# Cross-attention values with the transposed probabilities as weights, in a one-core transformer block

## The chip, the cores and the metric

One Trainium2 chip, one of its cores. The metric is the device time of one execution in microseconds (us). Engines are named as the profile names them: PE is TensorE's products, PEld its weight loads, DVE is VectorE, ACT ScalarE, POOL GpSimd, and SP the engine that issues the DMAs.

## The reference, cut to what matters

A block on x of (8, 256, 1024), float32: grouped-query self-attention with sign weights, cross-attention to a context of (8, 256, 1024), and a low-rank gated feed-forward part, each behind a layernorm and added to x. The part that matters here:

```python
C_q, C_kv = Q @ Wq_d, K @ Wkv_d                       # 1024 -> 128, 1024 -> 64
CqWqk = (C_q @ W_qk).reshape(b, n, 16, 64)
scores = einsum('bnhl,bkl->bhnk', CqWqk, C_kv) / 8
attn = softmax(scores, axis=-1)                       # 256 keys a sequence
V_up = (C_kv @ Wv_u).reshape(b, nkv, 16, 64)
out = einsum('bhnk,bkhd->bnhd', attn, V_up)           # added to x
```

## The kernel before

Three phases follow one another: self-attention, cross-attention, feed-forward. One list, `ORDER`, is written out by hand (`self_order`, `cross_order`, `ffn_order`), and every engine's program goes through it and emits its own instructions of each step, with semaphore waits ahead of them. So the place of a step in `ORDER` is its place in the queue of each engine that takes part in it, SP's and POOL's among them; an engine does nothing out of that order.

**Cross-attention** goes over four groups g of 512 tokens (two sequences b), and in each over eight units j, U = 8g + j: two heads (r = 0, 1) of 64 columns by two sequences, four "heads" n = 4U to 4U + 3 in the code's count, written k0 to k3 here. Steps of a group ahead of the heads: `lowq`, `xq` (queries of a unit), `lowkv`, `vup` (values). Then `attention_order` (L62) writes the heads. In the step of head n it puts, in this order:

- `score` of head n + 3: PE (L819), four products into one of three score banks; DVE takes the maximum (L1298).
- `flip` n: PE transposes the probabilities, four blocks of 128x128 (L831).
- `exp` n + 1: ACT (L1032), with the row sums. `evac` n: copy of the transposed probabilities to SBUF, `probT`, on ACT for odd n (L1041), on DVE for even n (L1306).
- what is left of the side pieces of the step before (`rest`), and the first part of this step's own. Side pieces of a unit: at k0 and k3 a `turn` (PE, L696) of the next group's tiles, whose `split` (high half by ACT L991, low half by DVE L1199, out of the same bank) comes one step later, at k1 and k0; at k0 the layernorm statistics of a tile (DVE L1187 to L1193, POOL L1473, L1475); at k1, for j up to 5, `xq` of unit j + 2 (PE L885), whose `xq_out` comes at k2: ACT L1063, DVE L1357, and four DMAs of SP into `xq_stack` (L1636), on which `score` of that unit's first head waits, at k1 of the next unit; at k3 the load of a tile. The last group has no turns and splits.
- the finish of the unit before (`finish`, L93): at k1 `xcopy`: ACT copies the bank `attn` (values, heads and columns on partitions, tokens along the free axis) to `xattnT` (L1078). At k2 `xfin`: PE turns it into one of two `proj` banks (four transposes, L904); then `xfin_out`: DVE multiplies by the reciprocal sums into `tmp` (L1382), POOL adds that to `x_group` (L1514), SP stores it (L1642) and reloads the slice of the unit before that for the next group (L1646).
- after odd heads, that is at k2 and at the next k0, `values` for b = 0 and b = 1 (L834 to L849).

`values` has the value columns as weights (128 keys x 64) and the transposed probabilities moving (256 queries). Its products for r = 0 and r = 1 go to the halves of the array's columns:

```python
t = pe.matmul(attn[r * XD:(r + 1) * XD, b * SEQ:(b + 1) * SEQ],
              xv[:, b * QT + kt, (2 * j + r) * XD:(2 * j + r + 1) * XD],   # weights
              probT[n % 6][:, kt * SEQ:(kt + 1) * SEQ], ..., tile_position=(0, r * XD))
```

The first `values` of a unit waits until `xcopy` of the unit before has read `attn` (`xcopied`). What a group's last unit leaves to finish (`late`) stands behind the next group's `lowq`, or at the end of the phase, which waits for the last stores. The `proj` banks are handed out in the order of `ORDER` (`bank_uses`) to all steps of the table `BANKED`, `turn`, `xq` and `xfin` among them. A float32 product is recorded as two pieces, each with its weight load; a transpose or a product of the type float32r as one. Line 707, which the prediction refers to, makes a float32 product with 128x128 weights of ones and 128 moving columns.

Of the kernel before, what the change touches and what calls it, by code (L numbers as in the profile page):

```python
# [5 lines left out]
F32 = mybir.dt.float32  # L6
# [55 lines left out]
def attention_order(first, heads, side, lead):  # L62
# [8 lines left out]
    for n in range(heads + 1):  # L71
        if n + AHEAD < heads:
            order.append(("score", first + n + AHEAD))
        if n < heads:
            order.append(("flip", first + n))
            if n + 1 < heads:
                order.append(("exp", first + n + 1))
            order.append(("evac", first + n))
        order += rest
        rest = []  # L80
        for piece in side.get(n, []):
            order.append(piece[0])
            rest += piece[1:]
        if finish:
            order += finish.pop(0)
        if n >= 1:
            m = n - 1
            if m % 2 == 1:
                order.append(("values", (first + m) // 2))
            if m % XUH == XUH - 1:  # L90
                unit = (first + m) // XUH
                order.append(("xend", unit))
                finish += [[("xcopy", unit)], [("xfin", unit), ("xfin_out", unit)]]  # L93
# [193 lines left out]
def ffn_order():  # L287
# [54 lines left out]
    for i in range(2 * TILES):  # L342
# [9 lines left out]
          "lowkv": "lowkv_out", "xq": "xq_out", "vup": "vup_out", "xfin": "xfin_out", "b1": "b1_out",  # L352
# [79 lines left out]
def build_program(nc, x, ctx_in, wq, qs, wk, ks, wv, vs, wo, os_, wq_d, w_qk, wkv_d, wv_u,  # L432
# [3 lines left out]
    def sb(name, shape, dt, where=ctx):  # L436
        return where.enter_context(nc.sbuf_tensor(name, shape, dt))

    def semaphore(name):
# [53 lines left out]
            for i, ph in enumerate("yc")}  # L493
# [10 lines left out]
    OTs = [sb(f"xattnT{i}", [P, GT], F32, mem) for i in range(2)]  # L504
# [34 lines left out]
             "xv_dve xv_act xrecip xcopied xnormed xadded "  # L539
# [21 lines left out]
    def copied_out(kind, *at):  # L561
# [25 lines left out]
        if kind == "xfin_out":  # L587
            return sem["xnormed"], at[0] + 1
# [76 lines left out]
    def tensor_program(e):  # L665
        pe = e.eng
        for kind, *at in ORDER:
# [166 lines left out]
            elif kind == "values":  # L834
# [5 lines left out]
                if b == 0 and U:  # L840
                    e.wait_ge(sem["xcopied"], U)
                for kt in range(QT):
                    for r in range(2):
                        n = 2 * s + r
                        e.wait_ge(evacuated[n % 2], n // 2 + 1)
                        t = pe.matmul(attn[r * XD:(r + 1) * XD, b * SEQ:(b + 1) * SEQ],  # L846
                                      xv[:, b * QT + kt, (2 * j + r) * XD:(2 * j + r + 1) * XD],
                                      probT[n % 6][:, kt * SEQ:(kt + 1) * SEQ], start=kt == 0, stop=kt == QT - 1,
                                      tile_position=(0, r * XD))  # L849
# [37 lines left out]
            elif kind == "vup":  # L887
# [9 lines left out]
                t.then_inc(full, 1)  # L897
            elif kind == "xfin":
                U = at[0]
                J, full, use = bank_of("xfin_out", U)  # L900
                e.wait_ge(sem["xcopied"], U + 1)
                bank_free(e, "xfin_out", U)
                for a in range(TILES):
                    t = pe.transpose(J[:, a * P:(a + 1) * P], OTs[U % 2][:, a * P:(a + 1) * P], ident[:, :])  # L904
# [60 lines left out]
    def scalar_program(e):  # L965
        act = e.eng
        for kind, *at in ORDER:
# [104 lines left out]
            elif kind == "xcopy":  # L1072
                U = at[0]
                e.wait_ge(sem["valued"], (U + 1) * GB)
                if U > 1:
                    _, full, use = bank_of("xfin_out", U - 2)
                    e.wait_ge(full, use + 1)
                act.activation(OTs[U % 2][:, :], attn[:, :], ACT.Copy).then_inc(sem["xcopied"], 1)  # L1078
# [72 lines left out]
    def vector_program(e):  # L1151
        dve = e.eng
        for kind, *at in ORDER:
# [220 lines left out]
            elif kind == "xfin_out":  # L1374
                U = at[0]
                J, full, use = bank_of("xfin_out", U)
                heads4 = lambda a: a.rearrange("p (a r d) -> p a r d", a=TILES, r=2)
                e.wait_ge(full, use + 1)
                e.wait_ge(sem["xrecip"], U + 1)
                if U > 1:  # L1380
                    e.wait_ge(sem["xadded"], U - 1)
                t = dve.tensor_tensor(  # L1382
                    heads4(tmp[U % 2][:, :]), heads4(J[:, :]),
# [351 lines left out]
```

## Time and profile before

| | |
|---|---|
| Median of 3 runs | 1601.66 us (1598.12 to 1612.58) |
| The profiled execution's own time | 1598.57 us |
| Its span | 1596.8 us |
| PE busy | 1409.5 us, 88% |
| DVE, ACT, POOL busy | 936.7, 707.6, 483.1 us |
| Mean granted TensorE clock | 0.958 |

The profile is of one execution. Busy time is the time in which an engine had at least one instruction at work; products on PE are pipelined, so the records of neighbours overlap and the last one's end is modelled. A wait is idle time of an engine ahead of an instruction, put down to what ended it. In the table by stretches PEclk is the granted clock, 1.00 being 2.4 GHz. The heads of cross-attention lie from about 745 to 1104 us.

### The profile page before, as it was taken

What the parts mean: (1) busy time and instruction counts of PE and PEld (TensorE: products, weight loads), DVE (VectorE), ACT (ScalarE), POOL (GpSimd) and SP (SyncE); (2) the same over time, 40 slices, a digit from 0 to 9 for tenths busy, and PEclk for the clock granted to TensorE, in tenths of its full rate; (3) what the DMA queues carried; (4) which work ended last, traced back from release to release, by engine and by line L of the source; (5) the groups of instructions that cost most, each with busy time, mean ns of one, the idle gap of its engine ahead of it and who ended that gap; (6) DMA issues with size and microseconds to landing.
All of it is one profiled execution on the core that took longest, in us unless ns stands there. A gap on an engine that the chain in (4) does not pass through costs nothing.

```text
span 1596.8 us, 22580 instructions
## 1 busy us (share of the span) xinstructions
PE 1409.5 (88%) x8423; PEld 989.6 (62%) x8423; DVE 936.7 (59%) x1643; ACT 707.6 (44%) x1584; POOL 483.1 (30%) x434
## 2 busy tenths in 40 slices
PE   5877899789978998687888989887899999999998
PEld 3545455545554555345766767675788888888886
DVE  5477555755565456454857758466374573673645
ACT  5164603441344124402765747475454444453442
POOL 2045402551254225611212112113252242252331
PEclk9998999899988998988999999998899999999999
DMA  5865454626451644136554636345610220220111
GB/s 185 115 117 128 94 84 97 114 41 114 99 108 29 113 107 61 41 139 178 145 146 106 176 90 171 93 106 155 234 55 1 78 81 1 79 80 0 67 66 53
DMA packets 94880, 157.54 MB, mean 99 GB/s; under 512 B 9910, under 2 KB 49076, under 8 KB 94772
## 3 DMA queue, kind: packets, MB, share of 16 engines
q1 hardware_dynamic: 94772, 156.11, 39.2%
q8 instruction: 67, 1.10, 0.3%
q14 instruction: 41, 0.34, 0.1%
HBM read 82.15 MB, written 25.17 MB: 67 GB/s over the span
## 4 chain that ended last, share of the span: by engine, by line
PE 67%; DVE 12%; DMA 8%; ACT 5%; issue 4%; SPq 3%; POOL 1%; DVEq 0%; ACTq 0%; POOLq 0%
PE bank L935 15%; PE bank L947 7%; PE bank L861 7%; PE bank L742 6%; PE bank L776 4%; DMA q_stack<-top_rows 3%; PE bank L920 3%; PE bank L696 3%; PE bank L756 3%; PE bank L875 3%; PE bank L789 2%; PE bank L819 2%; PE bank L960 2%; PE bank L846 2%; PE bank L802 2%
## 5 line engine op out<-in xcount | busy, mean ns | idle before, releaser
L1465 POOL TENSOR_TENSOR fold<-wide 128x512 f32<-128x512 f32 x128 | 163.0, 1274 | 321.0 <-ACT wide L1015 235.7
L1268 DVE TENSOR_REDUCE neg_top<-bank 128x2 f32<-128x512 f32 x256 | 171.3, 684 | 88.3 <-PE bank L756 87.6
L1015 ACT ACTIVATE wide<-bank 128x512 f32<-128x512 f32 x256 | 150.8, 596 | 146.7 <-PE bank L776 142.7
L776 PE MATMUL bank<-q_stack,k_stack 98*128 98x512 f32 x256 | 144.5, 567 | 61.3 <-DMA q_stack<-top_rows 59.9
L1537 POOL TENSOR_TENSOR v_lo<-v_all,v_hi 128x512 fp32r<-128x512 f32 x88 | 122.7, 1396 | 247.4 <-ACT v_hi L1100 247.4
L935 PE MATMUL bank<-pT_hi,v_hi 128*128 128x512 f32 x352 | 137.3, 390 | 2.6 <-POOL v_lo L1537 2.6
L935 PE MATMUL bank<-pT_hi,v_lo 128*128 128x512 f32 x352 | 137.1, 390 | 0.0
L935 PE MATMUL bank<-pT_lo,v_hi 128*128 128x512 f32 x352 | 137.0, 389 | 0.0
L1422 DVE SCALAR_TENSOR_TENSOR inner<-bank,b_cols,inner 128x512 f32<-128x512 f32 x88 | 66.0, 750 | 112.6 <-PE bank L935 109.3
L1032 ACT ACTIVATE wide<-bank,neg_max 128x256 f32<-128x256 f32 x256 | 120.0, 489 | 8.3 <-DVE neg_max L1298 8.3
L776 PEld LDWEIGHTS bank<-q_stack,k_stack 98*128 98x128 f32 x256 | 51.4, 202 | 106.5 <-DMA q_stack<-top_rows 71.2
L756 PEld LDWEIGHTS bank<-k_stack,q_stack 96*128 96x128 f32 x512 | 100.7, 203 | 24.7 <-DVE neg_top L1268 4.0
L1123 ACT ACTIVATE inner_hl<-inner 128x512 fp32r<-128x512 f32 x88 | 55.6, 632 | 135.3 <-DVE inner L1422 135.3
L947 PE MATMUL bank<-inner_hl,u_hi 128*128 128x512 f32 x352 | 111.4, 398 | 3.7 <-DVE inner_hl L1425 3.7
L756 PE MATMUL bank<-k_stack,q_stack 96*128 96x256 f32 x512 | 111.4, 305 | 3.3 <-DMA q_stack<-hi_lo 2.3
L696 PE MATMUL bank<-ident,xin 128*128 128x128 f32 x480 | 82.8, 305 | 31.7 <-DVE hT_lo L1199 8.7
L1298 DVE TENSOR_REDUCE neg_max<-bank 128x2 f32<-128x512 f32 x128 | 87.0, 685 | 38.1 <-PE bank L819 37.7
L742 PE MATMUL bank<-hT_hi,signs_qkv 128*128 128x512 f16 x256 | 103.3, 404 | 2.6 <-DVE hi_lo L1244 1.5
L861 PE MATMUL bank<-signs_o,attnT_hi 128*128 128x512 f16 x256 | 98.4, 384 | 5.8 <-POOL attnT_lo L1487 4.5
L742 PE MATMUL bank<-hT_lo,signs_qkv 128*128 128x512 f16 x256 | 101.0, 395 | 0.0
L1425 DVE TENSOR_TENSOR inner_hl<-inner,inner_hl 128x512 fp32r<-128x512 f32 x88 | 65.0, 738 | 61.4 <-ACT inner_hl L1123 61.4
L1514 POOL TENSOR_TENSOR x_group<-x_group,tmp 128x512 f32<-128x512 f32 x32 | 40.9, 1277 | 198.2 <-DVE tmp L1382 198.2
(176 smaller groups left out, 3106.5 us busy)
## 6 DMA issues: line engine op xcount, KB each, us to landing
q_stack<-hi_lo SPq DMA_DIRECT2D x96, 256.0 KB, 5.6
xin<-x_scratch SPq DMA_DIRECT2D x33, 512.0 KB, 4.5
xq_stack<-xhi_lo SPq DMA_DIRECT2D x128, 128.0 KB, 2.4
x_res<-in_x SPq DMA_DIRECT2D x19, 512.0 KB, 4.6
x_scratch<-x_res SPq DMA_DIRECT2D x16, 512.0 KB, 2.7
xin<-in_ctx SPq DMA_DIRECT2D x16, 512.0 KB, 4.6
x_group<-x_scratch SPq DMA_DIRECT2D x32, 256.0 KB, 3.5
x_scratch<-x_group SPq DMA_DIRECT2D x32, 256.0 KB, 2.6
```

The lines of the kernel that those rows point to most:

```text
L696: t = pe.transpose(J[:, i * P:(i + 1) * P], src[:, kb * P:(kb + 1) * P], ident[:, :])
L742: t = pe.matmul(J[:, :], sW[:, kb, tq * P:(tq + 1) * P], hT[p][:, kb, :], start=kb == 0 and p == 0, stop=kb == KB - 1 and p == 1)
L756: t = pe.matmul(tops[n % 2][:, a * SEQ:(a + 1) * SEQ], qst[U % Q_STACKS][0:SUB, r, b * SEQ + a * P:b * SEQ + (a + 1) * P], kst[0:SUB, tq, ...
L776: pe.matmul(tiles[m % 2][:, :], kst[0:SUB + 2, tq, b * SEQ + kt * P:b * SEQ + (kt + 1) * P], qst[U % Q_STACKS][0:SUB + 2, 2 * hp:2 * hp + ...
L861: t = pe.matmul(J[:, :], OT[p][:, tq, m * P:(m + 1) * P], sWo[:, tq, n * GT:(n + 1) * GT], start=tq == 0 and p == 0, stop=tq == KB - 1 and ...
L935: t = pe.matmul(G[:, :], v1s[W % 3][wp][:, s, r, :], pT[g % 2][ap][:, r, :], start=r == 0 and (wp, ap) == (0, 0), stop=r == RB - 1 and wp ...
L947: t = pe.matmul(z_banks[r][:, :], u2s[W % 3][wp][:, r, :], inner_hl[W % 2][:, ap, :], start=f == 0 and (wp, ap) == (0, 0), stop=f == FB - ...
L1015: act.activation(PT[m % PT_RING][:, :], tiles[m % 2][:, :], ACT.Exp).then_inc(sem["tile_exped"], 1)
L1032: t = act.activation(Pb[:, a * SEQ:(a + 1) * SEQ], S[:, a * SEQ:(a + 1) * SEQ], ACT.Exp, bias=mx[:, a:a + 1], accum_out=total)
L1268: dve.tensor_reduce(neg_top[U % 2][:, r, b, :], tops[n % 2][:, :].rearrange("p (a b) -> p a b", a=QT), AX.X, ALU.max, negate=True).then_in ...
L1465: pool.tensor_tensor(fold[f % FOLD_RING][:, :], PT[2 * f % PT_RING][:, :], PT[(2 * f + 1) % PT_RING][:, :], ALU.add).then_inc(sem["folded" ...
L1537: pool.tensor_tensor(lo[:, :, :, 0:n], inner_gu(f, n), hi[:, :, :, 0:n].bitcast(F32), ALU.subtract).then_inc(sem["iw_lo"], 1)
```

## The change

`values` swaps its operands: the transposed probabilities are the weights (128 keys x 128 queries) and the value columns move (64), so queries come out on the partitions. For each r, each half of the queries (`qt`) and each half of the keys (`kt`) there is one product, eight in a call where there were four, and they use all columns of the array. `xcopy`, `xfin`, the buffer `xattnT` and the `proj` bank of `xfin` are gone; `xfin_out` reads `attn` itself and stands where `xcopy` stood, at k1 in place of k2. The first `values` of a unit waits until `xfin_out` of the unit before has read the bank (`xnormed`).

```diff
--- before.py
+++ after.py
@@ -90,7 +90,7 @@
             if m % XUH == XUH - 1:
                 unit = (first + m) // XUH
                 order.append(("xend", unit))
-                finish += [[("xcopy", unit)], [("xfin", unit), ("xfin_out", unit)]]
+                finish.append([("xfin_out", unit)])
     late = rest
     for f in finish:
         late = late + f
@@ -349,7 +349,7 @@
 
 BANKED = {"scales": "scales_out", "sturn": "sevac", "turn": "split", "row_v": "row_v_out", "row_o": "row_o_out",
           "k": "k_out", "v": "v_out", "q": "q_out", "top": "top_out", "o": "o_out", "lowq": "lowq_out",
-          "lowkv": "lowkv_out", "xq": "xq_out", "vup": "vup_out", "xfin": "xfin_out", "b1": "b1_out",
+          "lowkv": "lowkv_out", "xq": "xq_out", "vup": "vup_out", "b1": "b1_out",
           "down": "down_out", "y": "y_out"}
 CHUNKED = ("q", "o", "down")
 
@@ -501,7 +501,6 @@
     xhl = [sb(f"xhi_lo{i}", [P, 2, GT], F32R, mem) for i in range(2)]
     xst = [sb(f"xq_stack{i}", [P, 2, GT], F32R, mem) for i in range(3)]
     xg = sb("x_group", [P, TILES, D], F32, mem)
-    OTs = [sb(f"xattnT{i}", [P, GT], F32, mem) for i in range(2)]
     xr = [sb(f"xrecip{i}", [P, 4, 2], F32, mem) for i in range(2)]
     mem.close()
     attn_mem.close()
@@ -536,7 +535,7 @@
              "v_norm ones_set pre_scored pre_maxed top_hi top_lo tiled tile_exped folded mixed mix_copied summed sum_turned "
              "recip recip_set attn_out attn_hi attn_lo o_dve scored maxed exped flipped valued "
              "raw_qd raw_kvd raw_qk raw_vu raw_hi raw_lo cq_hi cq_lo ckv_hi ckv_lo xstack_hi xstack_lo "
-             "xv_dve xv_act xrecip xcopied xnormed xadded "
+             "xv_dve xv_act xrecip xnormed xadded "
              "u2_zero b1_zero b1_landed b1_set b2_landed u1_hi u1_lo p_hi p_lo v2_hi v2_lo "
              "iw_zero iw_hi iw_lo dw_hi dw_lo gate_up silu inner inner_hi inner_lo z_done z_hi z_lo y_dve").split()
     sem = {n: semaphore(n) for n in names}
@@ -584,8 +583,6 @@
             return sem["xstack_lo"], XSTACK[(kind, *at)] + 1
         if kind == "vup_out":
             return sem["xv_act" if at[1] % 2 else "xv_dve"], 4 * at[0] + at[1] // 2 + 1
-        if kind == "xfin_out":
-            return sem["xnormed"], at[0] + 1
         if kind == "b1_out":
             return sem["b1_set"], 1
         if kind == "down_out":
@@ -838,15 +835,17 @@
                 e.wait_ge(sem["xv_dve"], 4 * (g + 1))
                 e.wait_ge(sem["xv_act"], 4 * (g + 1))
                 if b == 0 and U:
-                    e.wait_ge(sem["xcopied"], U)
-                for kt in range(QT):
-                    for r in range(2):
-                        n = 2 * s + r
-                        e.wait_ge(evacuated[n % 2], n // 2 + 1)
-                        t = pe.matmul(attn[r * XD:(r + 1) * XD, b * SEQ:(b + 1) * SEQ],
-                                      xv[:, b * QT + kt, (2 * j + r) * XD:(2 * j + r + 1) * XD],
-                                      probT[n % 6][:, kt * SEQ:(kt + 1) * SEQ], start=kt == 0, stop=kt == QT - 1,
-                                      tile_position=(0, r * XD))
+                    e.wait_ge(sem["xnormed"], U)
+                for r in range(2):
+                    n = 2 * s + r
+                    e.wait_ge(evacuated[n % 2], n // 2 + 1)
+                    for qt in range(QT):
+                        c = ((b * QT + qt) * 2 + r) * XD
+                        for kt in range(QT):
+                            t = pe.matmul(attn[:, c:c + XD],
+                                          probT[n % 6][:, kt * SEQ + qt * P:kt * SEQ + (qt + 1) * P],
+                                          xv[:, b * QT + kt, (2 * j + r) * XD:(2 * j + r + 1) * XD],
+                                          start=kt == 0, stop=kt == QT - 1)
                 t.then_inc(sem["valued"], 1)
             elif kind == "o":
                 g, i, c = at
@@ -894,14 +893,6 @@
                 for p in range(2):
                     t = pe.matmul(J[:, :], ckv[g % 2][:, p, m * P:(m + 1) * P], wvu[:, n * GT:(n + 1) * GT],
                                   start=p == 0, stop=p == 1)
-                t.then_inc(full, 1)
-            elif kind == "xfin":
-                U = at[0]
-                J, full, use = bank_of("xfin_out", U)
-                e.wait_ge(sem["xcopied"], U + 1)
-                bank_free(e, "xfin_out", U)
-                for a in range(TILES):
-                    t = pe.transpose(J[:, a * P:(a + 1) * P], OTs[U % 2][:, a * P:(a + 1) * P], ident[:, :])
                 t.then_inc(full, 1)
             elif kind == "b1":
                 J, full, use = bank_of("b1_out")
@@ -1069,13 +1060,6 @@
                     e.wait_ge(sem["valued"], g * XPAIRS * GB)
                 t = act.activation(xv[:, i // 2, GT:2 * GT], J[:, :], ACT.Copy)
                 t.then_inc(sem["xv_act"], 1)
-            elif kind == "xcopy":
-                U = at[0]
-                e.wait_ge(sem["valued"], (U + 1) * GB)
-                if U > 1:
-                    _, full, use = bank_of("xfin_out", U - 2)
-                    e.wait_ge(full, use + 1)
-                act.activation(OTs[U % 2][:, :], attn[:, :], ACT.Copy).then_inc(sem["xcopied"], 1)
             elif kind == "v2_load":
                 i = at[0]
                 buf, land, count = row_of("v2_load", i)
@@ -1373,14 +1357,13 @@
                 dve.reciprocal(xr[U % 2][:, :, :], row_sums[U % 3][:, :, 0:2]).then_inc(sem["xrecip"], 1)
             elif kind == "xfin_out":
                 U = at[0]
-                J, full, use = bank_of("xfin_out", U)
                 heads4 = lambda a: a.rearrange("p (a r d) -> p a r d", a=TILES, r=2)
-                e.wait_ge(full, use + 1)
+                e.wait_ge(sem["valued"], (U + 1) * GB)
                 e.wait_ge(sem["xrecip"], U + 1)
                 if U > 1:
                     e.wait_ge(sem["xadded"], U - 1)
                 t = dve.tensor_tensor(
-                    heads4(tmp[U % 2][:, :]), heads4(J[:, :]),
+                    heads4(tmp[U % 2][:, :]), heads4(attn[:, :]),
                     xr[U % 2][:, :, :].rearrange("p a (r o) -> p a r o", o=1).to_broadcast([P, TILES, 2, XD]),
                     ALU.mult)
                 t.then_inc(sem["xnormed"], 1)
```

## Rows read from the trace of the kernel before

**Rows 1.** Table by stretches: stretch, us, busy of PE, PEld, DVE, ACT, POOL, PEclk

```profile
475.00:540.00 65.00, 57.00 (x403) 30.90 (x400) 31.92 (x56) 27.52 (x49) 27.85 (x26) 0.87 0.41 69
765.00:1106.00 341.00, 303.75 (x2110) 231.79 (x2109) 226.94 (x416) 216.33 (x691) 66.11 (x61) 1.00 0.47 128
```

**Rows 2.** Table of waits, 765 to 1106: us in total, times, longest

```profile
PE bank L904 <- ACT xattnT L1078: 11.0, 12, 1.2
PE bank L904 <- DVE actT_lo L1199: 5.9, 15, 0.4
PE bank L819 <- DMA xq_stack<-xhi_lo: 6.0, 12, 0.8
```

**Rows 3.** Timeline of a unit, all engines: start us, us, line, operation [idle before]

```profile
788.53 0.73 PE L819 MATMUL bank<-ckv,xq_stack 128*128 128x256 f32 x4 [0.23 <-DMA xq_stack<-xhi_lo]
...
789.74 0.60 ACT L1041 ACTIVATE wide<-bank 128x512 f32<-128x512 f32 x1 [1.30 <-PE bank L831]
...
790.72 0.60 PE L831 MATMUL bank<-ident,wide 128*128 128x128 f32 x4
...
790.86 0.69 DVE L1199 TENSOR_TENSOR actT_lo<-bank,actT_hi 128x512 fp32r<-128x512 f32 x1 [0.86 <-ACT actT_hi L991]
...
791.46 0.68 DVE L1298 TENSOR_REDUCE neg_max<-bank 128x2 f32<-128x512 f32 x1
...
791.69 0.63 PE L904 MATMUL bank<-ident,xattnT 128*128 128x128 f32 x4 [0.38 <-DVE actT_lo L1199]
...
792.25 1.08 PE L846 MATMUL bank<-wide,xv_all 128*64 128x256 f32 x8
...
792.78 2.39 SPq L1636 DMA_DIRECT2D xq_stack<-xhi_lo  x4
...
793.27 0.74 PE L819 MATMUL bank<-ckv,xq_stack 128*128 128x256 f32 x4
...
793.35 0.68 DVE L1382 TENSOR_TENSOR tmp<-bank,xrecip 128x512 f32<-128x512 f32 x1
...
794.11 1.28 POOL L1514 TENSOR_TENSOR x_group<-x_group,tmp 128x512 f32<-128x512 f32 x1 [7.69 <-DVE tmp L1382]
...
795.41 0.38 SPq L1642 DMA_DIRECT2D x_scratch<-x_group  x1
...
795.84 0.56 SPq L1646 DMA_DIRECT2D x_group<-x_scratch  x1
...
797.17 0.74 PE L819 MATMUL bank<-ckv,xq_stack 128*128 128x256 f32 x4
```

**Rows 4.** Timeline of PEld at 44 us, and source views of L707, L846 (min/median/max)

```profile
44.45 0.52 PEld L707 LDWEIGHTS bank<-tmp,ones 128*128 128x128 f32 x4 [2.31 <-issue]
...
L707 PEld LDWEIGHTS bank<-tmp,ones x20: 186/238/338, 44.5 to 205.9; 128*128 128x128 f32 x20
...
L846 PEld LDWEIGHTS bank<-wide,xv_all x512: 132/136/137, 765.7 to 1102.2; 128*64 128x64 f32 x171
```

**Rows 5.** Timelines of SP and PE, first and last group

```profile
783.82 2.80 SPq L1636 DMA_DIRECT2D xq_stack<-xhi_lo  x4
...
1057.90 0.74 PE L819 MATMUL bank<-ckv,xq_stack 128*128 128x256 f32 x4 [0.68 <-DMA xq_stack<-xhi_lo]
...
1061.67 2.39 SPq L1636 DMA_DIRECT2D xq_stack<-xhi_lo  x4
...
1065.94 0.74 PE L819 MATMUL bank<-ckv,xq_stack 128*128 128x256 f32 x4 [0.77 <-DMA xq_stack<-xhi_lo]
```

**Rows 6.** Timeline of PE, the unit with j = 6

```profile
814.97 0.74 PE L819 MATMUL bank<-ckv,xq_stack 128*128 128x256 f32 x4
...
818.40 1.08 PE L846 MATMUL bank<-wide,xv_all 128*64 128x256 f32 x8
```

**Rows 7.** Timeline at the end of the heads

```profile
1102.81 0.60 ACT L1078 ACTIVATE xattnT<-bank 128x512 f32<-128x512 f32 x1 [1.17 <-PE bank L846]
...
1104.15 0.69 DVE L1382 TENSOR_TENSOR tmp<-bank,xrecip 128x512 f32<-128x512 f32 x1 [3.91 <-PE bank L904]
```

## The prediction

> **What bounds the kernel now.** The table by stretches comes first [rows 1]. The change acts only in the cross-attention heads, 765 to 1106 us, and there TensorE is busy 303.75 of 341 us, VectorE 226.94 and ScalarE 216.33, at a granted clock of 1.00. So TensorE's own work is most of the time, and 37 us of its idle time is what waits can give back. Next the table of waits for the same stretch [rows 2]: TensorE sat 11.0 us for ScalarE's copy `xcopy` and 5.9 us for VectorE's `actT_lo`, both in front of `xfin` (L904), and 6.0 us for the DMAs that fill `xq_stack`. Last the timeline of one unit [rows 3], because it says what is late *behind* each wait. I call a unit's four heads k0 to k3, as in the section on the kernel, and count t from the start of the `score` at k1 (788.53).
>
> In that unit the flip of k1 ends, ScalarE evacuates it (t = 1.21), then does its half of the `split`, VectorE does the other half (t = 2.33) and is free for the next at t = 2.93; `xfin` runs at t = 3.16, the first `values` at 3.72, and k1 of the next unit at 8.64. Over three units the period is (814.97 - 788.53) / 3 = 8.81 us [rows 3, 6].
>
> **The values call, 64 times.** Now 4 products, recorded as 8 pieces because a float32 product is two passes: 8 pieces of 256 columns last 1.08 us with their tail and the next work starts 1.02 us after them (793.27 - 792.25) [rows 3]. Two of them run side by side, one per half of the array's columns. After: 8 products, 16 pieces, each with 128x128 weights and 64 moving columns. In moving columns the two tie: 8 x 256 in pairs is 1,024, 16 x 64 is 1,024. What grows is the weights: from 8 loads of 64 columns to 16 loads of 128. The trace has that very load, float32 128x128 for a true product, in L707 at full clock: four loads in 0.52 us, each at least 186 ns long, so one every (0.52 - 0.19) / 3 = 0.11 us [rows 4]. There 128 columns also move per piece (line 707 writes 128 columns), so the row doesn't say which of the two sets the 0.11. Bounds: below, the load is hidden and 64 columns take half of 0.11, 0.055 a piece; above, load and move don't overlap at all, 0.11 + 0.055 = 0.165. A 64-column load lasts 136 ns and the 128-column one 186 [rows 4], so 64 more columns cost 50 ns, and 128 columns some 0.10: the load by itself is near 0.11. I take 0.11, the nearest row: 16 x 0.11 = 1.76 us, so +0.74 a call; 64 calls would be +47.4 us if nothing else moved.
>
> The Trainium skill, "TensorE: Matmul & The Clock Gate", section on LDWEIGHTS, has the load take P / 1.2 ns for P weight columns and gives the fast load only to types other than FP32. By it a piece takes at least 107 ns and the call 1.71 us, and the trace agrees as far as L707's 0.11 goes. The same page's section on the back-to-back issue gap has pairs of load and product at N = 128 at about 81 ns; by that the call would be 1.30 us. The first speaks against this change, and L707 sides with it.
>
> **xfin and xcopy, 32 times.** `xfin` holds TensorE from 791.69 to 792.25, 0.56 us, so 32 x 0.56 = 17.9 us, and the waits in front of it are 11.0 + 5.9 = 16.9 us [rows 2, 3]: 34.8 us that the edit seems to free. But `values` for b = 0 must now wait for `xnormed`, which is VectorE's `xfin_out`, where it waited for ScalarE's copy. `xfin_out` is moved one head earlier, to k1, behind that head's `split`. VectorE is free for it at t = 2.93 and it lasts 0.68, so it ends at 3.61 [rows 3]. TensorE arrives far earlier: the flip of k2 starts at t = 2.19 and takes 0.44, so 2.63. Values then start at about 3.66 against 3.72 now. The freed 0.56 us and the old 0.4 us idle become one wait of 1.0 us, since the chain flip, evacuation, two halves of split stays and `xfin_out` takes the place of `xcopy` and `xfin`. Queued behind the waiting `values` is all of TensorE's order, and everyone waits for that. In units without an `xq` (j = 6 and 7) values now start at 818.40 - 814.97 = 3.43 [rows 6], so there 3.66 is 0.23 later. ScalarE loses 0.6 us a unit, which nobody waited for beyond `xfin`. The freed `proj` bank relieves nothing that shows more than 2 us in all.
>
> **The move past SP's queue.** `xfin_out` at k1 now stands ahead of `xq_out` (k2) on SP, which takes its queue in order. Now SP starts the four `xq_stack` DMAs at 792.78 (t = 4.25), and the store and reload follow at 795.41 and 795.84 [rows 3]. After, SP first waits for POOL's add: `xfin_out` ends at 3.61, the add starts 0.08 later (793.35 + 0.68 = 794.03 against 794.11) and lasts 1.28, so 4.97; the store's issue 0.38, the reload's 0.56, 0.05 between: the stack's DMAs start at t = 6.03. From their start to the `score` that waits for them it is 788.53 - 783.82 = 4.71 at worst and 1065.94 - 1061.67 = 4.27 in the last group, where SP is otherwise quiet [rows 3, 5]. So next k1 cannot start before 10.3 to 10.7; I take 10.5, the middle. TensorE's own path is 3.66 + (797.17 - 792.25) + 2 x 0.74 = 10.06, so it is the DMAs that are late next, by 0.4.
>
> **The sum, by intervals from k1 to k1.**
> First three groups, j = 1 to 5, fifteen intervals: 10.5 - 8.81 = +1.69, so +25.4 (+18.8 if TensorE's path decides, +28.4 at 10.7).
> Their j = 0, three: no `xfin_out` falls into them; 2 x 0.74 less the 0.23 of DMA wait it covers, +3.8.
> Their j = 6 and 7, six: 1.48 + 0.23 = 1.7, +10.2.
> Last group: no splits, and it is bound by the stack's DMAs at 1065.94 - 1057.90 = 8.04 [rows 5]. Without splits `xfin_out` follows the maximum of k1 and ends near t = 2.1, before TensorE is there (2.6); there `xfin` really goes. Five intervals: 8.04 - 0.72 (the mean of the two DMA waits shown) - 0.56 + 1.48 = 8.24, +1.0, and the SP chain (2.1 + 0.08 + 1.28 + 0.4 + 4.27 = 8.1) fits under it except in the first, which still has a reload, +0.4. j = 0: 1.48 - 0.7 = +0.8. j = 6 and 7: 2.96 less `xfin` twice and an estimated 0.3 of wait ahead of each, +1.2. Together +3.4.
> Group boundaries: `xfin` no longer sits between `lowq` and `xq`, an estimated 0.2 of its 0.56 each, since the copy that follows `lowq` stays: -0.6. End: VectorE's last `tmp` starts with what was the copy, 1104.15 - 1102.81 [rows 7] = -1.3, and the feed-forward part waits for exactly that store.
> Sum 25.4 + 3.8 + 10.2 + 3.4 - 0.6 - 1.3 = +40.9. The profiled execution took 1598.6 us (span 1596.8), so 1639.5; it lies 3.1 us below the median of the three runs, 1601.7, within their spread.
>
> **Rivals.**
> *Loads cheaper, chain holds.* At 0.055 a piece values cost what they do now. For: no row has a float32 load with fewer than 128 columns moving behind it. Against: the 50 ns between the two load lengths. The fifteen intervals stay at 10.5, since the path through VectorE, POOL and SP doesn't depend on values: +25.4, six times 0.23 = +1.4, last group about -0.9, -1.9: 1623. Chance 13%.
> *TensorE's amount of work alone decides* (the other side). The chain flip, split, `xfin_out` would have to finish before TensorE, in all 28 units' k1. For: TensorE is the busiest engine, and ScalarE is relieved. Then the edit gives back 34.8 + 6.0 = 40.8 us and costs 64 x (16r - 1.02) at r us a piece: at r = 0.11 +6.6, 1605; at r = 0.08 -24, 1574; it turns faster below r = 0.104. Against: in the unit shown ScalarE had no work before its evacuation, so its relief moves nothing. Chance 6%.
> *Load and move one after the other.* 0.165 a piece, V = 2.6, so TensorE's path is 11.8: fifteen times 2.95, three times 2.95, six times 3.4, last group 16.9, ends -1.9: +88.6, 1687. Against: L707 has 128-column moves and loads in 0.11 together. 6%.
> *The clock falls.* The heads now run at 1.00; the self-attention stretch 475 to 540, with TensorE busy 57.00 of 65 us, has 0.87 [rows 1]. The new waits (1.0 plus 0.4 us a unit) bring the heads near that busy share. At 0.87 the some 333 us of TensorE work grow by up to 50; half of it hidden or all of it: 1664 to 1689. 6%.
> The forecast has the remaining 69%, by itself from 1630 to 1650 (a piece of 0.10 to 0.117 us, stack DMAs of 4.2 to 4.8 us).
>
> **How the numbers follow.** From 1614 to 1662 the range takes in the forecast and the rival of cheap loads with some us of its own, and leaves out the rest. One per cent, 16 us, is about what a measurement of this kernel can tell from no change. Slower by more: the forecast, the two dearer rivals, and over half of the cheap loads, 87%. Within: 9%. Faster: what is left of the other side, 4%.
>
> **What would show it.** Values: 16 pieces in 1.8 to 1.9 us, loads 0.11 apart. The table of waits: TensorE's `values` (L846 moved a few lines) waiting for VectorE's `tmp`, some 1.0 us in each of 21 units and nearly none in the last group; and the `score` waiting for the `xq_stack` DMAs by 0.4 in the first three groups, some 6 us in all, with SP's `x_scratch` store ahead of them. Period of units j = 1 to 5 about 10.4 against 8.8, last group 8.3 against 8.0. Wrong would be: loads under 0.08 apart, values starting at t = 2.6, SP issuing the stack before the store, or a clock row under 1.00 between 765 and 1146.

## The result, and the profile after

The changed kernel took 1680.53 us (median of 4 runs, 1674.11 to 1682.52), the kernel before 1606.56 us in the same comparison (4 runs): a ratio of 1.0465, with a 95% interval of 1.0437 to 1.0494. It is slower, as forecast, but by nearly twice as much as forecast (+40.9 us), and above the range. The profiled execution took 1679.93 us against 1598.57 before, +81.4. Its page, first the busy time by engine, then the granted clock in 40 slices of the span:

```profile
PE 1469.3 (88%) x8807; PEld 1087.2 (65%) x8807; DVE 936.6 (56%) x1643; ACT 692.1 (41%) x1552; POOL 483.0 (29%) x434
...
PEclk9998999799988998879999999799799999999999
```

PE is busy 60 us longer, ACT 15 us shorter (`xcopy` is gone). Where the 81.4 us lie is found with two marks of the timeline: from the first `xq` of the heads to the last `tmp` it is 763.91 to 1104.15 before (340.2 us) and 770.28 to 1186.34 after (416.1 us), so +75.8 in the heads. The heads begin 6.4 us later, in stages whose code is the same (among the profiled executions here that start varies from 763.3 to 773.4), and what follows them is 0.9 us shorter. The table by stretches (columns as in [rows 1]) for the heads, and for two places within them:

```profile
770.00:1187.00 417.00, 355.50 (x2503) 327.75 (x2501) 227.21 (x420) 201.75 (x660) 65.39 (x61) 0.93 0.37 105
809.00:824.00 15.00, 10.98 (x78) 10.29 (x78) 6.46 (x11) 6.30 (x21) 1.26 (x1) 0.89 0.49 139
1080.00:1100.00 20.00, 17.33 (x73) 15.00 (x74) 4.54 (x8) 3.06 (x6) 2.54 (x2) 0.74 0.10 29
```

Before, the heads had 303.75 us of PE in 341 at a clock of 1.00 [rows 1]. After, PE is busy 52 us longer, but it is also idle 61.5 us instead of 37, and the clock is 0.93: one of the signs by which the prediction said it would be wrong. Within the heads, from that first `xq` to the end of the last `tmp`, there are now 14 stretches at the lower level, 1.2 GHz, together 58.0 us; before there was none. (Low-clock time is counted in this way for every run below.) The table of waits for 745 to 1190, which answers to [rows 2]:

```profile
PE bank L816 <- DMA xq_stack<-xhi_lo: 24.2, 17, 2.6
PE bank L845 <- DVE tmp L1365: 21.7, 20, 2.1
```

The `values` call (L845) waits for VectorE's `tmp` 20 times by about 1.1 us, as forecast. The `score` (L816) waits for the stack's DMAs four times as long in all as the 6 us forecast. One unit shows both, and answers to [rows 3] (timeline, all engines; t from the `score` at k1, 798.88):

```profile
798.88 0.74 PE L816 MATMUL bank<-ckv,xq_stack 128*128 128x256 f32 x4 [0.63 <-DMA xq_stack<-xhi_lo]
...
801.21 0.69 DVE L1183 TENSOR_TENSOR actT_lo<-bank,actT_hi 128x512 fp32r<-128x512 f32 x1 [0.86 <-ACT actT_hi L982]
...
801.82 0.68 DVE L1365 TENSOR_TENSOR tmp<-bank,xrecip 128x512 f32<-128x512 f32 x1
...
802.55 1.86 PEld L845 LDWEIGHTS bank<-xv_all,wide 128*128 128x128 f32 x16 [1.14 <-DVE tmp L1365]
802.56 2.00 PE L845 MATMUL bank<-xv_all,wide 128*128 128x64 f32 x16 [0.90 <-DVE tmp L1365]
802.58 1.27 POOL L1497 TENSOR_TENSOR x_group<-x_group,tmp 128x512 f32<-128x512 f32 x1 [9.52 <-DVE tmp L1365]
...
803.87 0.37 SPq L1625 DMA_DIRECT2D x_scratch<-x_group  x1
804.29 0.52 SPq L1629 DMA_DIRECT2D x_group<-x_scratch  x1
...
804.90 2.43 SPq L1619 DMA_DIRECT2D xq_stack<-xhi_lo  x4
...
807.14 1.90 PE L845 MATMUL bank<-xv_all,wide 128*128 128x64 f32 x16
...
811.46 1.22 PE L816 MATMUL bank<-ckv,xq_stack 128*128 128x256 f32 x4 [2.42 <-DMA xq_stack<-xhi_lo]
```

Values start at t = 3.68, SP issues the stack at t = 6.02; the forecast had 3.66 and 6.03. Then it parts from the forecast: the stack lands 6.56 us after its first issue (811.46 - 804.90), not 4.27 to 4.71, and the `score` that has waited for it takes 1.22 us for what takes 0.74 at the full clock. The period of this unit is 12.58 us, the third longest of its kind; over the fifteen units j = 1 to 5 of the first three groups the mean is 11.58 (by the starts of `score` at k1), where 10.5 was forecast and 8.76 stood before.

### The profile page after: what moved, and what is told of

It reads as the page before. It is cut to its first block, busy times and chain, and to the rows that moved or that the text cites. A ratio compares the mean times of both kernels' runs of the same rounds, so it can differ in the third digit from the quotient of the medians.

```text
span 1678.1 us, 23282 instructions
## 1 busy us (share of the span) xinstructions
PE 1469.3 (88%) x8807; PEld 1087.2 (65%) x8807; DVE 936.6 (56%) x1643; ACT 692.1 (41%) x1552; POOL 483.0 (29%) x434
## 4 chain that ended last, share of the span: by engine, by line
PE 63%; DVE 12%; issue 11%; DMA 7%; POOL 3%; ACT 3%; SPq 2%; DVEq 0%; POOLq 0%; ACTq 0%
PE bank L926 14%; PE bank L938 7%; PE bank L860 6%; PE bank L739 6%; PE bank L773 4%; PE bank L845 3%; DMA q_stack<-top_rows 3%; PE bank L753 3%; PE bank L911 3%; PE bank L693 2%; PE bank L786 2%; PE bank L799 2%; PE bank L951 2%; PE bank L874 2%; DVE bn L1171 2%
## 5 line engine op out<-in xcount | busy, mean ns | idle before, releaser
L845 PE MATMUL bank<-xv_all,wide 128*128 128x64 f32 x1024 | 131.0, 284 | 21.7 <-DVE tmp L1365 21.7
L845 PEld LDWEIGHTS bank<-xv_all,wide 128*128 128x128 f32 x1024 | 127.1, 202 | 26.6 <-DVE tmp L1365 26.5
L816 PE MATMUL bank<-ckv,xq_stack 128*128 128x256 f32 x512 | 94.3, 312 | 25.0 <-DMA xq_stack<-xhi_lo 24.2
```

Of the source, the lines that this page charges most:

```text
L845: t = pe.matmul(attn[:, c:c + XD], probT[n % 6][:, kt * SEQ + qt * P:kt * SEQ + (qt + 1) * P], xv[:, b * QT + kt, (2 * j + r) * XD:(2 * j ...
```

## Experiments

The theory before the first ones: two chains make the loss. In the first, `values` waits for `xfin_out`, which stands behind the `split` on VectorE. In the second, SP's store and reload stand ahead of the stack's DMAs. The low clock follows from the waits. Its rival: the longer `values` is most of the loss by itself. All diffs are against the changed kernel unless another is named. The kernel before took 1602.13, 1604.74 and 1602.39 us (medians) beside the three batches; ratios are to it. The changed kernel was not run again beside them, so what a run gains on it is given by the medians and, in brackets, by the ratios.

**The two halves of the change, each alone.** `swap_only`: the new operands, but `xcopy` and `xfin` kept, in their old places.

```diff
-                finish.append([("xfin_out", unit)])
+                finish += [[("xcopy", unit)], [("xfin", unit), ("xfin_out", unit)]]
...
-                    e.wait_ge(sem["xnormed"], U)
+                    e.wait_ge(sem["xcopied"], U)
...
+            elif kind == "xfin":
+                    t = pe.transpose(J[:, a * P:(a + 1) * P], OTs[U % 2][:, a * P:(a + 1) * P], ident[:, :])
...
+                act.activation(OTs[U % 2][:, :], attn[:, :], ACT.Copy).then_inc(sem["xcopied"], 1)
```

> The kernel before with only the operands of values swapped; xcopy, xfin and the waits stay (the transposes then turn a block that is already the right way round, which costs the same and makes the output another one). Theory of two chains: values cost 0.80 us more in each of 64 calls, +51, less the 6 us of waits for the stack's DMAs that this covers: +45, 1645 to 1655, with TensorE's clock near 1.00 in the heads and the score waiting under 3 us for the stack. Rival, that operands and clock are the whole of it: the swap alone brings more than the changed kernel's +74, since the removal gives something back: +90 to +110, 1690 to 1715, the clock at 0.93 or below.

1636.69 us, ratio 1.0213 (1.017 to 1.0257), +34.6 us; below the expected 1645 to 1655. From its table of waits, 765 to 1190:

```profile
PE bank L906 <- ACT xattnT L1080: 11.2, 12, 1.2
...
PE bank L906 <- DVE actT_lo L1201: 5.7, 15, 0.4
```

The waits ahead of `xfin` are what they were [rows 2], the 6 us of stack waits are covered, and low-clock time in the heads is 3.4 us. So the operands alone, in the old order, make about half of the loss, and the rival, which had them above all of it, falls. `removal_only`: the order and the waits of the changed kernel with the old products.

```diff
-                for r in range(2):
...
-                            t = pe.matmul(attn[:, c:c + XD],
-                                          probT[n % 6][:, kt * SEQ + qt * P:kt * SEQ + (qt + 1) * P],
+                for kt in range(QT):
...
+                        t = pe.matmul(attn[r * XD:(r + 1) * XD, b * SEQ:(b + 1) * SEQ],
+                                      xv[:, b * QT + kt, (2 * j + r) * XD:(2 * j + r + 1) * XD],
...
```

> The changed kernel with the old operands of values (value columns as weights); no xcopy, no xfin, and xfin_out at k1 on the untransposed bank, so the output is another one. It has 34.8 us less of TensorE work and waits by the rows of before. Theory of two chains: slower than before all the same, by 15 to 30 us (1617 to 1632), with periods of 10.4 to 11 us in units j = 1 to 5 of the first three groups, the score waiting 30 us or more for the stack's DMAs. Rival: faster than before by 18 to 35 us, 1566 to 1585.

1661.53 us, ratio 1.037 (1.034 to 1.04). It came out above both expectations: a kernel that takes work away from the one before, adds none and moves `xfin_out` to k1 is 59 us slower. In its table of waits, 765 to 1190, the stack's DMAs alone cost 52.1 us:

```profile
PE bank L816 <- DMA xq_stack<-xhi_lo: 52.1, 24, 4.0
PE bank L843 <- DVE tmp L1363: 18.1, 15, 2.1
```

and its timelines of SP and PE say why. With store and reload ahead the stack lands in 5.42 us (810.23 - 804.81); TensorE stood idle for 2.66 us of it:

```profile
803.79 0.37 SPq L1623 DMA_DIRECT2D x_scratch<-x_group  x1
804.20 0.51 SPq L1627 DMA_DIRECT2D x_group<-x_scratch  x1
804.81 2.43 SPq L1617 DMA_DIRECT2D xq_stack<-xhi_lo  x4
...
810.23 0.74 PE L816 MATMUL bank<-ckv,xq_stack 128*128 128x256 f32 x4 [2.66 <-DMA xq_stack<-xhi_lo]
```

**The second chain.** `store_behind` leaves `xfin_out` at k1 and puts SP's store and reload one head later, behind the stack's DMAs.

```diff
-                finish.append([("xfin_out", unit)])
+                finish += [[("xfin_out", unit)], [("xstore", unit)]]
...
-            elif kind == "xfin_out":
+            elif kind == "xstore":
```

> The changed kernel with SP's store and reload put one head later, behind the stack's four DMAs, where they were; nothing else moves. Theory of two chains: the score's wait for the stack falls from 24.2 us to under 5, the clock in the heads rises from 0.93 to 0.97 or more, 20 to 40 us less than the changed kernel: 1640 to 1660. The wait of values for tmp stays near 22 us. Rival: within 5 us of the changed kernel.

1647.9 us, ratio 1.0285 (1.0241 to 1.0328): 33 us of the loss gone (29). The wait for the stack falls from 21.9 us (765 to 1190) to 1.8, that for `tmp` is 25.4 us, low-clock time falls from 58.0 to 34.1 us. The clock in its heads is 0.96, short of the expected 0.97. `reload_behind` splits this further: only the reload goes behind, the store stays ahead.

```diff
-                finish.append([("xfin_out", unit)])
+                finish += [[("xfin_out", unit)], [("xreload", unit)]]
...
+            elif kind == "xreload":
```

> The changed kernel with only SP's reload (x_group from x_scratch, 256 KB) behind the stack's DMAs; the store stays ahead. If the bytes of the reload ahead of the stack's on the DMA rings are what makes the landing 5.2 to 6.6 us in place of 4.2 to 4.8: the score's wait for the stack falls from 24.2 to under 8 and the time by 12 to 30 us, 1650 to 1668, and from the start of the four issues to the score it is 4.2 to 4.8 again. If it is only SP's late start: the start is 0.6 us earlier in fifteen units, the wait falls by some 9 us and the time by 8 to 12.

1661.49 us, ratio 1.034 (1.0299 to 1.0381), 19 us below the changed kernel (20), as the first of the two accounts in the expectation has it. Its timelines of SP and PE (the `score` has no wait, so this is an upper limit of the landing):

```profile
906.97 0.36 SPq L1625 DMA_DIRECT2D x_scratch<-x_group  x1
907.43 2.39 SPq L1619 DMA_DIRECT2D xq_stack<-xhi_lo  x4
909.87 0.59 SPq L1631 DMA_DIRECT2D x_group<-x_scratch  x1
...
911.95 0.72 PE L816 MATMUL bank<-ckv,xq_stack 128*128 128x256 f32 x4
```

With the store alone ahead the stack is there within 4.52 us (911.95 - 907.43), and the wait for it is 5.7 us in all. So it is mainly the reload in front, not the store, that lengthens the landing. But six landings of 5.0 to 5.9 us are left even here; their cause is open.

**The first chain.** `norm_first` puts `xfin_out` ahead of the `split` within k1, and leaves SP's order as it is.

```diff
+        if finish:
+            order += finish.pop(0)
...
-        if finish:
-            order += finish.pop(0)
```

> The changed kernel with xfin_out one place earlier within k1, ahead of the split of the turned tile, on VectorE, POOL and SP alike. Theory of two chains: VectorE ends it at t = 2.1, before TensorE is at values, so that wait falls from 21.7 us to under 5; POOL's add and SP's store come 1.5 us earlier too, so the score's wait for the stack falls from 24.2 to under 12. 25 to 45 us less than the changed kernel: 1635 to 1655. Rival, the wait only goes elsewhere (to the split, which frees the bank): within 10 us.

1632.63 us, ratio 1.0186 (1.0155 to 1.0217): 48 us gone (45). The wait of `values` for `tmp` falls from 21.7 to 0.9 us, low-clock time from 58.0 to 17.1 us. Two numbers of the expectation missed: the time is a little below its range, and the stack wait, expected under 12 us, stays at 21.1 us. The stack is issued earlier, but the period shrinks with it, and the landing behind the reload stays long (timelines of SP and PE):

```profile
905.98 0.89 SPq L1629 DMA_DIRECT2D x_group<-x_scratch  x1
906.97 2.42 SPq L1619 DMA_DIRECT2D xq_stack<-xhi_lo  x4
...
912.23 0.50 PE L816 MATMUL bank<-ckv,xq_stack 128*128 128x256 f32 x2 [1.08 <-DMA xq_stack<-xhi_lo]
```

**Both chains loosened.** Two kernels failed to do what their expectations say. `both_orders` joins the diffs of `norm_first` and `store_behind`, `removal_both` is that with the old products. But the finish then stands ahead of all else in k2 as well, so SP's store and reload are still ahead of the stack.

> store_behind and norm_first together: xfin_out ahead of the split, and SP's store and reload behind the stack's DMAs. What is left of the change is then the operands (now measured at 1.70 us a call in stream, 0.68 more than before, 64 x 0.68 = 43.5) against xcopy, xfin and all their waits (34.8 and 6.0 us by the rows of before). Theory of two chains: both waits under 5 us in all, the clock in the heads near 1.00, and 1600 to 1613, within 1% of the kernel before. Rival, that the two orders repair the same 30 to 45 us and don't add: 1628 to 1640.

> both_orders with the old operands of values: the removal of xcopy and xfin alone, without either chain; its output is another one, since nothing turns the result. Theory: faster than before, by 15 to 30 us (1572 to 1590); less than the 40.8 us of the rows, since units j = 1 to 5 then meet the stack's DMAs at a period of 8.0 to 8.6. Rival, that the removal is worth nothing even without the chains: within 8 us of before.

`both_orders`, 1631.34 us, ratio 1.0157 (1.0128 to 1.0186), with 16.0 us of stack waits, is a second `norm_first`; that it lies in the range of its rival says nothing for the rival. `removal_both`, 1623.65 us, ratio 1.0111 (1.0079 to 1.0142), with 40.9 us of stack waits in 22 units, is once more a kernel with less work that is slower than the one before. The order was then put right in `two_orders`, the changed kernel's computation with `xfin_out` ahead of the `split` and the store and reload behind the stack:

```diff
...
+        if finish:
+            order += finish.pop(0)
...
-        if finish:
-            order += finish.pop(0)
+        if stores:
+            order += stores.pop(0)
...
+                stores += [[], [("xstore", unit)]]
```

> What both_orders was meant to be: there the finish was put ahead of the whole rest, so that SP's store and reload still stood ahead of the stack's DMAs at k2 (its trace has store, reload, stack), and it was norm_first a second time. Here xfin_out stands ahead of the split at k1 and SP's store and reload behind the stack's four DMAs at k2. Theory of two chains: both waits of TensorE under 5 us in all, the low clock in the heads under 15 us, and 1600 to 1613, within 1% of the kernel before. Rival, that the two orders repair the same microseconds: 1625 to 1635, as norm_first.

1609.28 us (median), ratio 1.0034 (1.0012 to 1.0056). Nearly the whole loss is gone with every one of the 1,024 new pieces still there. One unit in its timelines of PE, DVE and SP, and the stretch of the heads:

```profile
891.87 0.72 PE L819 MATMUL bank<-ckv,xq_stack 128*128 128x256 f32 x4
...
893.24 0.68 DVE L1368 TENSOR_TENSOR tmp<-bank,xrecip 128x512 f32<-128x512 f32 x1
...
894.48 1.90 PE L848 MATMUL bank<-xv_all,wide 128*128 128x64 f32 x16
...
895.62 2.39 SPq L1622 DMA_DIRECT2D xq_stack<-xhi_lo  x4
898.05 0.59 SPq L1628 DMA_DIRECT2D x_scratch<-x_group  x1
898.69 0.55 SPq L1632 DMA_DIRECT2D x_group<-x_scratch  x1
...
900.67 0.72 PE L819 MATMUL bank<-ckv,xq_stack 128*128 128x256 f32 x4
```

```profile
765.00:1109.00 344.00, 321.07 (x2491) 299.79 (x2489) 225.22 (x416) 200.28 (x658) 65.45 (x61) 1.00 0.47 127
```

Values start 2.61 us after k1 and wait for nothing; the period is 8.80 us where it was 8.81. The stack wait is 1.9 us, that for `tmp` 1.2, and there is no low-clock time in the heads. PE does 17 us more work than before in a stretch 3 us longer. `removal_two` is this with the old products:

> two_orders with the old operands of values (the output is another one, nothing turns the result): the removal of xcopy and xfin without either chain. Theory: 1572 to 1592, faster than before by less than the 40.8 us of the rows, since units j = 1 to 5 then meet the stack's DMAs at a period of 8.0 to 8.6. Rival, that the removal is worth nothing: within 8 us of before.

1584.99 us, ratio 0.9883 (0.9854 to 0.9911). This is what taking out `xfin` and `xcopy` is worth when nothing is moved in the way: 17 us, not the 40.8 of the rows. Half of the difference is the wait for the stack's DMAs, in 24 units (table of waits, 765 to 1190), which the 40.8 had at nothing; the other half, some 12 us, is not accounted for:

```profile
PE bank L819 <- DMA xq_stack<-xhi_lo: 11.9, 24, 1.5
```

With nothing ahead of them they land 4.2 to 4.3 us after their issue in most units, 5.0 at most.

**What a piece of `values` costs.** `moving_128` is `both_orders` with 128 moving columns in place of 64; `weights_64` is `two_orders` with 64 weight columns (half of the queries left out). Each has one time only.

```diff
-                        c = ((b * QT + qt) * 2 + r) * XD
+                        c = (b * QT + qt) * P
...
-                            t = pe.matmul(attn[:, c:c + XD],
+                            t = pe.matmul(attn[:, c:c + P],
...
-                                          xv[:, b * QT + kt, (2 * j + r) * XD:(2 * j + r + 1) * XD],
+                                          xv[:, b * QT + kt, 2 * j * XD:(2 * j + 2) * XD],
```

```diff
-                            t = pe.matmul(attn[:, c:c + XD],
-                                          probT[n % 6][:, kt * SEQ + qt * P:kt * SEQ + (qt + 1) * P],
+                            t = pe.matmul(attn[0:XD, c:c + XD],
+                                          probT[n % 6][:, kt * SEQ + qt * P:kt * SEQ + qt * P + XD],
```

> both_orders with 128 moving columns (both heads' values) in every piece of values in place of 64, so each head's result is overwritten in part by the next and the output is another one. If the weight loads set the pace of a piece, a call still lasts 1.70 us give or take 0.1, and the time is that of both_orders within 8 us. If load and move add up, a call grows by 16 x 0.05 = 0.85 us and the time by 50.

> two_orders with weights of 64 columns (half of each block of probabilities) in every piece of values, 64 moving columns as before; the other half of the queries is left out. Same number of pieces and the same moving columns. If the weight load sets the pace, a piece takes 0.055 to 0.075 us and a call about 1.0 to 1.2 us in place of 1.70, and the time falls by 25 to 45 us below two_orders. If a piece costs a fixed 0.1 us whatever it loads, the call stays at 1.6 to 1.7 us and the time within 8 us.

From the timeline of PE in each, the call and what follows it, first `moving_128`:

```profile
895.34 1.95 PE L845 MATMUL bank<-xv_all,wide 128*128 128x128 f32 x16
897.04 0.72 PE L816 MATMUL bank<-ckv,xq_stack 128*128 128x256 f32 x4
```

then `weights_64`:

```profile
886.80 1.15 PE L848 MATMUL bank<-xv_all,wide 128*64 128x64 f32 x16
887.87 0.73 PE L819 MATMUL bank<-ckv,xq_stack 128*128 128x256 f32 x4
```

Twice the moving columns leave the call at 1.70 us (897.04 - 895.34), the same as with 64; the time was 1637.24 us against 1631.34 for `both_orders`, one time against a median. Half the weight columns bring it to 1.07 us. Within a call the records of the loads start 0.112 us apart with 128 weight columns, with 64 and with 128 moving columns alike, and 0.058 us apart with 64 weight columns. So the number of weight columns sets the pace of a piece, and the moving columns don't. For the call the expectation of `weights_64` came true, for the whole kernel it missed: 1591.6 us, 18 us below `two_orders` (11.5 by the spans, 1601.3 and 1589.8), where 25 to 45 was expected, in part because TensorE then waits 13.6 us for the stack's DMAs, in 21 units.

The Trainium skill, "TensorE: Matmul & The Clock Gate", in its section on LDWEIGHTS, has the load last its number of columns divided by 1.2, in ns: 107 ns for 128 and 53 for 64. The traces agree with it to some 5 ns, at 0.112 and 0.058 us from load to load. The section of the same page on the back-to-back issue gap has pairs at N = 128 at about 81 ns; for these float32 pieces `moving_128` shows 0.112 us.

## Why the prediction was right in direction and short in size

**The values call: right.** 1.76 us was forecast. In a stream it is 1.70 us, and 1.80 after a wait: in the unit shown, the next `score` starts at 804.36, and the call at 802.56. `moving_128` and `weights_64` confirm the reason given, that the load sets the pace, and the loads are 0.112 us apart where 0.11 was taken.

**xfin and xcopy, and the wait for `xnormed`: right.** Values at t = 3.68 against 3.66; 21.7 us of waits in 20 calls against 1.0 us in each of 21. `norm_first`, which takes that wait away, shows that it matters: 48 us, more than twice the wait itself, since low-clock time goes with it (58.0 to 17.1 us) and the stack is issued earlier.

**Where the forecast fell short, by intervals.** The sum of the prediction can be held against the `score` at k1 of every unit (before and after, starts from the timelines of PE; us more than before):

| Stretch | Forecast | Measured |
|---|---|---|
| First three groups, j = 1 to 5 | +25.4 | +42.3 |
| Their j = 0 | +3.8 | +2.6 |
| Their j = 6 and 7, with the three group boundaries | +9.6 | +22.9 |
| Last group, j = 0 to 5 | +2.2 | +8.2 |
| Its j = 6 and 7 and the end | -0.1 | -0.2 |
| Sum | +40.9 | +75.8 |

**The move past SP's queue: the place right, the term mis-sized.** The first step that failed is the landing of the stack's DMAs, 4.27 to 4.71 us: "So next k1 cannot start before 10.3 to 10.7; I take 10.5, the middle", with the `score` waiting "by 0.4 in the first three groups, some 6 us in all". The start of these DMAs was right (6.02 against 6.03). But in both rows that it took for the landing SP had issued nothing in the 4.9 us ahead of them [rows 3, 5]. In the 13 units of the first three groups of the changed kernel where a wait shows the landing, the issue of the reload stands directly ahead, and it took 4.46 once and 4.96 to 6.61 otherwise, 5.44 on the mean. Against the 4.49 in the middle of the forecast's two rows that is 0.95 us later in each of fifteen intervals, by this estimate 14 of the 16.9 us by which the first line of the table is short. `removal_only`, `reload_behind` and `store_behind` show that the cause is what stands ahead on the queue. That the reload's bytes are still on their way when the stack's are to move is the obvious reading; no run tells bytes from anything else that the reload brings.

The trace of before had rows with the reload directly ahead, at the stack for the first unit of each group, and from the second group on no `score` waited for it; the forecast didn't use them. Timeline of SP and source view of L1636 for one (840.0 to 842.3), then the same view of the changed kernel for the unit shown above, and that of before for all 32 stacks (745 to 1190):

```profile
839.27 0.36 SPq L1642 DMA_DIRECT2D x_scratch<-x_group  x1
839.67 0.51 SPq L1646 DMA_DIRECT2D x_group<-x_scratch  x1
840.28 2.44 SPq L1636 DMA_DIRECT2D xq_stack<-xhi_lo  x4
DMA to landing us min/median/max: 3.2/3.3/3.9
...
DMA to landing us min/median/max: 3.2/3.3/4.7
...
DMA to landing us min/median/max: 2.2/2.4/5.3
```

Each of the four DMAs takes 3.2 us or more there, where the median of all is 2.4, about as much more as the missing 0.95 us. (There the next unit's four DMAs follow at once, so the row is not quite the same case.)

**The last group: wrong.** The forecast had SP's chain fit under TensorE's path there "except in the first". `score` waited 1.06, 1.39 and 1.70 us for it, in three units, 4 of the 6 us by which that line is short. In the first of them nothing stood ahead of the stack, in the last only the store.

**The clock: the rival came with the forecast.** The second step that failed is that the likeliest case had the lower clock at nothing. It stood at 6%, as another case beside the forecast, yet its own argument was that the forecast's waits would bring it on. So it was no alternative, and had to be priced into the likeliest case once waits of 1.4 us a unit were in that case. Its price shows in the third line of the table, from k1 of the unit with j = 6 to k1 of the next group's j = 0: no `score` waits for the stack inside these stretches, they are 13.3 us over the forecast, and 33.9 of the 58.0 us of low clock lie in them. Table by stretches, the sum of the three (in the changed kernel 835.27 to 883.91, 951.52 to 999.32 and 1065.85 to 1116.68), in the changed kernel, in `store_behind` (34.1 us of low clock) and in `norm_first` (3.4 us), which run the same products in them:

```profile
sum 147.27, PE 119.05 PEld 101.29 DVE 57.28 ACT 48.75 POOL 14.92; mean PE 39.68 PEld 33.76 DVE 19.09 ACT 16.25 POOL 4.97
sum 147.22, PE 118.98 PEld 100.49 DVE 57.40 ACT 48.75 POOL 14.93; mean PE 39.66 PEld 33.50 DVE 19.13 ACT 16.25 POOL 4.97
sum 122.60, PE 104.25 PEld 87.69 DVE 57.39 ACT 48.43 POOL 14.94; mean PE 34.75 PEld 29.23 DVE 19.13 ACT 16.14 POOL 4.98
```

TensorE is busy 14.8 us longer for the same products, about half of the 30.5 us more of low clock, and idle 9.9 us longer, about its waits for `tmp` there (10.4 us, none in `norm_first`). So wait and clock add up there. With 14 us for the landings, 13 for the clock at the boundaries and 4 in the last group, 31 of the 34.9 us by which the forecast was short have a place and a cause; the rest is open. No run held the waits and took the clock away, so that the waits bring the lower clock on is shown only in that the two go together: 58.0 us of low clock in the changed kernel, 34.1 and 17.1 with one chain loosened, none with both, none before.

**The rival "work alone decides": wrong for this kernel, right for `two_orders`.** At 0.11 us a piece it had +6.6 us. With both chains loosened the ratio is 1.0034, which is 5.5 us. That it came so near is in part luck, for its parts were off by more than its sum. The operands alone cost 34.6 us, not 47.4 (6 us of stack waits were covered by them); the removal alone gives 17.4 (`removal_two`), not 40.8; and together they cost less than 34.6 - 17.4 = 17, since the longer `values` fills the 11.9 us that `removal_two` waits for the stack (1.9 in `two_orders`). By the order of the steps: without the chains the removal saves 17 us, with them it costs 59. The forecast had both chains, and it had rightly put the loss down to them; it had sized the second by the wrong rows, and left out the clock that came with them.

No kernel here beats the one before with its whole computation: `two_orders` comes within 0.34% of it.

## What to carry to other kernels

A step that is moved takes its DMAs along, past everything on the queue of the engine that issues them; when the start is worked out right, the landing must still be read from a row where the same transfers stand ahead, even from one for which nobody waits, and if there is none, its upper end is open. A wait added in a stretch that runs at the full clock is to be priced twice, by itself and by the lower clock it may bring, in the same case and not in a rival. And before giving up an edit for the waits it makes, write out the order again: here two moves of one step each brought the ratio from 1.0465 to 1.0034.

## What the runs showed of the hardware that was not expected

- Four DMAs of 128 KB each into `xq_stack` from one queue landed in 4.2 to 4.3 us in most units with nothing just ahead (`removal_two`; within 4.52 behind a store alone in the unit of `reload_behind` shown), and in 4.96 to 6.61 (4.46 once) with a reload of 256 KB issued 0.5 to 1.2 us before them. Why three of the changed kernel's 13 are at 6.56 to 6.61 and not near 5.2 stays open, and so does why some took 5.0 us and more with no reload just ahead (1.70 us of wait in the last group).
- After a wait of 2.42 us the granted clock was at its lower level, 1.2 GHz, for some 3 us: the `score` took 1.22 us for 0.74. A load of 128 columns lasted 186 to 193 ns in `two_orders`, whose heads ran at the full clock, and up to 338 ns in the changed kernel.
- The spacing of the float32 pieces didn't depend on 64 or 128 moving columns (0.112 us both times, 1.70 for a call of 16), only on the weight columns (0.058 us and 1.07 with 64).
